# First edge stage: the masked product reads the transposed rows from PSUM, and the transposition stands ahead of the outer products

## What is computed

```python
layer_input = jax.nn.relu(xn)
msg = layer_input[node_in] @ w1 + b1
msg = jax.nn.relu(_bn(msg, g_msg, be_msg, m_msg, v_msg))
kern = jax.nn.relu(edge_input @ kw1 + kb1) @ kw2 + kb2      # 32 hidden values for each edge
kern = kern.reshape(-1, H + 1, H)
msg = jnp.einsum('ejk,ek->ej', kern[:, 1:, :], msg) + kern[:, 0, :]
update = jax.ops.segment_sum(msg * edge_weight[:, None], node_out, num_segments=N)
```

## Time and profile before

| | us |
|---|---|
| median of 3 runs | 1812.79 |
| lowest and highest | 1805.26, 1816.29 |
| the profiled execution | 1820.72 |
| its span, first to last instruction | 1818.9 |
| PE busy in the span | 1412.1 (78%) |
| GpSimd (POOL) busy | 1013.0 (56%) |
| VectorE (DVE) busy | 978.6 (54%) |
| ScalarE (ACT) busy | 557.6 (31%) |

### The profile page before, as it was taken

How to read it: one execution, slowest core, us unless ns; L and a number is a source line. 1 busy time by engine, 2 the same in 40 slices (tenths; PEclk the granted TensorE clock), 3 DMA queues, 4 the chain that set the end, 5 groups by cost and what they waited for, 6 DMA issues and landing times.

```text
span 1818.9 us, 32058 instructions
## 1 busy us (share of the span) xinstructions
PE 1412.1 (78%) x9726; PEld 813.6 (45%) x9726; DVE 978.6 (54%) x2349; ACT 557.6 (31%) x1467; POOL 1013.0 (56%) x1008
## 2 busy tenths in 40 slices
PE   3577767777777776569869988888888888885899
PEld 1245545445544445345534433333333333373458
DVE  4444444444433333464436666666666666655763
ACT  2233333332333332135313333333333333212420
POOL 0677777777777777200017777777777777400000
PEclk9678888887788877789889999999999999996999
DMA  6322223232232322021013333333333333200001
GB/s 193 99 71 71 72 71 74 69 77 72 72 77 73 77 66 66 18 110 47 0 47 108 112 110 113 110 113 111 111 112 112 112 111 111 79 15 0 1 9 37
DMA packets 77717, 141.28 MB, mean 78 GB/s; under 512 B 24426, under 2 KB 32810, under 8 KB 77096
## 3 DMA queue, kind: packets, MB, share of 16 engines
q0 software_dynamic: 40128, 81.99, 17.2%
q1 hardware_dynamic: 37480, 57.93, 10.5%
HBM read 135.17 MB, written 4.67 MB: 77 GB/s over the span
## 4 chain that ended last, share of the span: by engine, by line
POOL 39%; PE 25%; issue 22%; DVE 6%; DMA 5%; ACT 1%; DVEq 1%; SPq 0%; POOLq 0%; PEldq 0%; ACTq 0%
POOL ring L413 21%; POOL arena L424 18%; DMA ring<-mtab,src 4%; PE ps L1037 3%; PE ps L868 3%; PE ps L1028 3%; PE ps L980 2%; PE ps L726 2%; PE ps L659 1%; PE ps L918 1%; PE ps L877 1%; DVE small L1055 1%; DVE arena L1330 1%; PE ps L739 1%; DMA arena<-utab,src 1%
## 5 line engine op out<-in xcount | busy, mean ns | idle before, releaser
L424 POOL DMA_INDIRECT arena<-utab,src x500 | 473.3, 947 | 356.3 <-DVEq L1290 202.5
L413 POOL DMA_INDIRECT ring<-mtab,src x500 | 537.6, 1075 | 205.5 <-issue 197.0
L1166 DVE TENSOR_TENSOR arena<-ring 128x1024 f32<-128x1024 f32 x125 | 153.3, 1227 | 345.2 <-PE ps L726 344.9
L918 PE MATMUL ps<-arena 128*128 128x512 f32 (+1 forms) x386 | 221.6, 656 | 11.9 <-DMA arena<-in_rbf 9.9
L1330 DVE TENSOR_TENSOR arena<-ps,arena 128x768 f32<-128x768 f32 x252 | 228.2, 947 | 0.0
L585 ACT ACTIVATE arena<-ps 128x512 f32<-128x512 f32 x193 | 115.2, 597 | 313.7 <-PE ps L918 311.1
L717 PE MATMUL ps<-ring 128*32 128x97 f32 x1000 | 52.4, 286 | 196.4 <-DMA ring<-mtab,src 196.0
L937 PE MATMUL ps<-arena 128*32 128x512 f32 x1008 | 134.2, 604 | 67.5 <-DVE arena L1330 67.4
L726 PE MATMUL ps<-arena,ring 128*64 128x128 f32 x2000 | 184.0, 333 | 0.0
L1328 DVE TENSOR_TENSOR arena<-ps,arena 128x512 f32<-128x512 f32 x126 | 87.1, 691 | 143.4 <-DMA arena<-utab,src 123.5
L726 PEld LDWEIGHTS ps<-arena,ring 128*64 128x64 f32 x2000 | 154.6, 170 | 11.8 <-issue 5.9
(11 more groups left out here) (219 smaller groups left out, 1862.6 us busy)
## 6 DMA issues: line engine op xcount, KB each, us to landing
arena<-in_eaT SPq DMA_DIRECT2D x125, 256.0 KB
ring<-mtab,src POOLq DMA_INDIRECT x500
arena<-utab,src POOLq DMA_INDIRECT x500
arena<-in_rbf SPq DMA_DIRECT2D x66, 64.0 KB
ring<-in_fw SPq DMA_DIRECT2D x2, 1024.0 KB, 6.7
utab<-arena SPq DMA_DIRECT2D x1, 2048.0 KB, 7.5
XT<-in_xT SPq DMA_DIRECT2D x2, 1000.0 KB
arena<-in_x SPq DMA_DIRECT2D x1, 1920.0 KB, 9.4
```

The source lines that it names most:

```text
L413: pool.indirect_dma_start(MR[:, n % 4, k, 0:H], None, mtab, bass.IndirectOffsetOnAxis(ap=src[:, 4 * n + k:4 * n + k + 1], axis=0)).then_in ...
L424: pool.indirect_dma_start(G1[:, n % NSLOT, k, :], None, utab, bass.IndirectOffsetOnAxis(ap=src[:, 4 * n + k:4 * n + k + 1], axis=0)).then_ ...
L918: pe.matmul(ps[:, 0, :], w, x, start=True, stop=True).then_inc(S["s_mlp"], 1)
L1166: dve.tensor_tensor(RM[:, n % 2, :, :, :], MR[:, n % 4, :, H + 1:].unsqueeze(3).broadcast_to([P, 4, KH, WIN]), SW[:, b % 2, 4 * k:4 * k + ...
```

## The change

VectorE's masked product takes its first input from PSUM bank 1, as TensorE's transposition left it, and no longer from `MR`. ScalarE's copy into `MR` stays, since `affine` reads it. Because VectorE now reads bank 1, the next transposition into that bank waits for the masked product (`s_mask`), and since `s_mask` now starts at one, the wait in `affine` counts one more. In the loops of TensorE and ScalarE the transposition and the copy of step n+2 move from the head of iteration n to the place just ahead of the outer products.

```diff
@@ ScalarE's loop @@
                 for n in range(-3, QT + 7):
-                    if 0 <= n + 2 < QT:
-                        edges(j, n + 2)
                     mix(j, n)
                     if n + 3 < QT:
                         relu(j, n + 3)
@@
                     if n >= 10 and n % QB == 0:
                         contracted(j, n // QB - 2)
+                    if 0 <= n + 2 < QT:
+                        edges(j, n + 2)
                     if 0 <= n < QT:
                         outer(j, n)
@@ TensorE, edge_rows @@
                 pe.wait_ge(S["s_relu"], j * QT + n + 2)
                 pe.wait_ge(S["s_rc"], j * QT + n + 1)
+                pe.wait_ge(S["s_mask"], j * QT + n + 1)
                 pe.transpose(ps[:, 1, 0:P], RT[:, n % 2, :], ident).then_inc(S["s_tr"], 1)
@@ TensorE, affine @@
-                    pe.wait_ge(S["s_mask"], j * QT + n + 1)
+                    pe.wait_ge(S["s_mask"], j * QT + n + 2)
@@ TensorE's loop @@
                 for n in range(-3, QT + 6):
-                    if 0 <= n + 2 < QT:
-                        edge_rows(j, n + 2)
                     if 0 <= n < QT + 2:
                         affine(j, n, 0)
                     mix(j, n)
@@
                     if 0 <= b < NB and k < 3:
                         contract(j, b, k)
+                    if 0 <= n + 2 < QT:
+                        edge_rows(j, n + 2)
                     if 0 <= n < QT:
                         outer(j, n)
@@ VectorE @@
             dve.sem_inc(S["s_rmw"], 1)
+            dve.sem_inc(S["s_mask"], 1)
@@ VectorE, masks @@
                     dve.tensor_tensor(RM[:, n % 2, :, :, :],
-                                      MR[:, n % 4, :, H + 1:].unsqueeze(3).broadcast_to([P, 4, KH, WIN]),
+                                      ps[:, 1, 0:P].rearrange("p (t q) -> p t q", t=4).unsqueeze(3).broadcast_to([P, 4, KH, WIN]),
                                       SW[:, b % 2, 4 * k:4 * k + 4, 0:WIN].unsqueeze(2).broadcast_to([P, 4, KH, WIN]),
                                       ALU.mult).then_inc(S["s_mask"], 1)
```

## The result

| | before | after |
|---|---|---|
| median, first sitting | 1811.05 us (1805.26 to 1816.29, 4 runs) | 1760.95 us (1759.10 to 1761.96, 4 runs) |
| the profiled execution | 1820.72 us | 1760.44 us |
| its span | 1818.9 us | 1758.6 us |

The ratio is 0.9723, with a 95% interval of 0.9691 to 0.9755: 50 us less, between 44 and 56. A second sitting gave 1811.79 us (9 runs) against 1761.11 us (5 runs), ratio 0.9722 (0.9701 to 0.9742).

A forecast was written before the change was run, and what follows sets the result against it. The first edge stage was taken to be bound by 500 successive GpSimd gathers, some lengthened by masks. Terms of -59.5 and +3.3 gave -56 us, so 1812.8 became 1757 us, range 1744 to 1780, leaving out the four rivals.

The forecast's parts named there:

- The bound: First edge stage, 689.60 us: 500 GpSimd gathers one after the other, with the three compute engines following.
- The main term: First edge stage: gathers that start inside a mask are no longer lengthened once it reads PSUM, -59.5 us.
- the price of 0: A mask with one input in PSUM holds no gather, judged from the second edge stage's products; 0 us.
- The gathers' next obstacle: The LayerNorm products in the mixing part lengthen relieved gathers, 6 us against 2.7 today: +3.3 us, at worst +24.
- Sum: -59.5 + 3.3 = -56 us, from a median of 1812.8 to 1757 us.
- The sign: Profile after, first edge stage: gathers at a mean of about 0.95 us, 474 to 480 us busy.
- The mask's duration: VectorE's 1024-column masked product from PSUM would take 1.21 us, against 1.227 from SBUF.
- The transposition's place and its wait: On TensorE, 0.33 to 0.48 us a step ahead of the outer products, covered by 9.6 us slot slack: 0.
- Rival 1: The mask holds gathers all the same, since its other input and output are in SBUF; 1812 us, chance 0.04.
- rival 2: The mask was never the cause; they share only the moment at which outer products end; 1812 us, chance 0.02.
- Rivals 3 and 4: Half-rate PSUM read with TensorE's low clock, 1797 us at most, chance 0.06; or the new loop bounds, 1844, chance 0.04.
- Rival 4: The loop of outer products, mask and transposition becomes the bound; a 3.7 us mask gives 1844 us; chance 0.04.

The follow-up runs named there:

- the run with the source without the order: Changed kernel with the transposition and ScalarE's copy back at the head of the iteration, mask still reading PSUM; 1768.25 us, ratio 0.9793.
- one more product: Changed kernel plus one 128x512 product a step with both inputs in SBUF, ahead of the mask; 1774.11 us in one run.
- the run with the order alone: Changed kernel with the masked product reading MR in SBUF again, transposition and copy left in their new place; 1820.33 us, ratio 1.0061.
- the run with 3.65 us of masks: Changed kernel with the masked product computed three times from PSUM, twice into unused columns; 1848.34 us in one run.
- two masks: Changed kernel with the masked product computed twice from PSUM, once into unused columns; 2206.47 and 2204.42 us on two slow chips.

## Why the prediction was right

The forecast was 1757 us in a range of 1744 to 1780, and 1761 was measured.

- *The bound.* That the stage is a row of 500 gathers was right: the stage shrank by as much as GpSimd's busy time, 56.1 us, with the compute engines' work unchanged.
- *The main term*, -59.5 us for gathers held by masks: measured, 59.5 of lengthening in gathers that start inside a mask went to 0. The step that carried it, from the second stage's products with one input in PSUM to a product of another length and pattern, held: the run with the source put back brings the lengthening back, and the run with the inputs exchanged shows that either input may be the one in PSUM. One reading under this term was off: counted over the trace again, 246 gathers of the second stage begin inside one of its two products, not 263. None of the 246 takes over 0.96 us, so the price of 0 stands as well on the right number.
- *The gathers' next obstacle*, +3.3 us: the mixing part's products went from 2.7 to 5.7 us of lengthening, +3.0. How closely that agrees is in part luck: it was 5.2 in the changed kernel's second trace, 4.7 in the run with the source without the order, and 8.1 with one more product.
- *Sum.* -56 us against -56.1 in the stage. The sign that I named for the gathers, 474 to 480 us busy, was too narrow: 481.4 was measured, and the sum itself asks for just that (537.5 - 56 = 481.5). For the median I carried the 56 over from one profiled execution, and there 50 were measured, with 56 at the interval's edge. The profiled execution of before was slower than any in the timed set (1820.7 against 1805 to 1816), and 4 us of the two spans' difference lie outside the stage. How many gathers are caught changes with how they fall on the masks (62.1 us in the run with the order alone, 59.5 in the kernel before); how much it changes between executions of the kernel before no run here shows.
- *The mask's duration*, 1.21 us: 1.224. The eightfold repeat of a PSUM element costs nothing against the same repeat from SBUF (1.227).
- *The transposition's place and its wait*, 0 behind the slots' slack: right, with 7.2 us left in the tightest case and 3.2 us of waits on TensorE. I counted the slack from the outer products' end; the 0.8 us that a waiting gather needs behind it belong off, which changes nothing here. The run with the old place shows what I had not priced: there the same wait comes in every step, and uses the slack up.
- *Rival 1 and rival 2* fell with the 123 gathers. *Rivals 3 and 4* wanted a mask of 2.45 and 3.7 us, and it took 1.22. Rival 4's sum was right: it had 1844 us for a mask of 3.7 us, and the run with 3.65 us of masks took 1848.

## What to carry to other kernels

Where GpSimd's gathers set the pace, compare the mean duration of a gather with its median. If the mean is higher, look at what VectorE runs when the long ones start. In this kernel a fp32 product with both inputs in SBUF holds a gather that starts inside it until 0.13 us before its own end; a plain fp32 copy from SBUF to SBUF holds those under way too; and a product with one of its inputs in PSUM holds none. The remedy may leave the duration of VectorE's instruction as it was. A PSUM bank that gets a second reader must be kept until that reader is done, so put the next write to it as late as its own users allow.

## What the runs showed of the hardware that I had not expected

- A fp32 copy from SBUF to SBUF and a gather hold each other in both directions, also in the middle: a gather that was 0.49 us under way became 1.30 us, and a copy that began 0.52 us into a gather took 0.94 us instead of 0.69.
- With TensorE waiting 1.49 us behind each set of outer products (the source without the order), its granted clock over the stage was 0.93, and its busy time 425.4 us, against 0.87 and 490.3 in the changed kernel for the same matmuls. Why, I did not test.
- On two chips the kernel before took 2179.4 and 2178.2 us. In the second run with two masks, on one of them, rows in order of time:

```profile
341.70 1.98 PE L727 MATMUL ps<-arena,ring 128*64 128x128 f32 x16
...
345.01 1.22 DVE L1168 TENSOR_TENSOR arena<-ps,ring 128x1024 f32<-128x1024 f32 x1 [2.02 <-PE ps L727]
```

The outer products end at 343.68 by their record and the mask that waits for them starts at 345.01, 1.3 us later, with VectorE idle; in the changed kernel elsewhere the same step takes 0.12 us. VectorE isn't what is late: the trace has the semaphore's step at 344.91, 0.09 us before the mask, as in the changed kernel. It is that step which comes 1.2 us after the matmuls' recorded end, with a median of 1.5 us over the run, against 0.02 us in the changed kernel. The ends of matmuls are modelled in a profile, so either TensorE ended later than its record says or the count arrived late. Which of the two stays open.
